# Eight of sixteen terms of a head-attention sum taken over by identity products; an exponent bias on another engine; re-ordered queues

## The reference, cut to what matters

```
x = x + attn(layernorm(x))         # head attention, below
x = x + xattn(layernorm(x), ctx)   # 16 heads, all 2048 keys, fake-quantised
x = x + ffn(layernorm(x))          # 8 experts, top 2, and a shared one
```

```
scores = einsum('bshd,bstd->bsht', q, k) / sqrt(16)   # h, t: heads; d: 16 features
probs  = softmax(scores, axis=-1)
attn   = einsum('bsht,bstd->bshd', probs, v) @ Wo.T
```

## Time and profile before

| | |
|---|---|
| median of 3 runs | 1065.17 us (1061.33 to 1065.57) |
| the profiled execution | 1068.14 us, span 1065.7 us |
| PE busy | 722.0 us (68%), 7072 products |
| DVE busy | 906.5 us (85%), 1841 instructions |
| ACT busy | 737.3 us (69%), 989 |
| POOL busy | 746.9 us (70%), 728 |
| mean granted TensorE clock | 0.838 |

### The profile page before, as it was taken

The page is one execution under the profiler, slowest core; times in us unless marked ns, Lnnn a source line. Parts: engine busy times, 40 slices in busy tenths (PEclk is TensorE's granted clock), DMA queues, the critical chain, the costliest instruction groups (busy, mean ns, idle before and its releaser), DMA issues. The chain is left out here.

```text
span 1065.7 us, 21210 instructions
## 1 busy us (share of the span) xinstructions
PE 722.0 (68%) x7072; PEld 388.6 (36%) x7072; DVE 906.5 (85%) x1841; ACT 737.3 (69%) x989; POOL 746.9 (70%) x728
## 2 busy tenths in 40 slices
PE   6966647666675867675776758576667767675674
PEld 4543323333342524343332425243333324242333
DVE  3887769989888899989898989899888989999851
ACT  2644656868677776868686877778686868878742
POOL 6688987787786778787886868787878868730000
PEclk9975777888896978889897989888878979798965
DMA  6012767979698896979797999979697979999981
GB/s 225 1 40 70 133 119 140 186 115 192 128 176 147 150 173 127 187 114 198 120 194 144 160 168 146 190 121 188 129 179 115 192 150 169 172 167 182 162 161 25
DMA packets 574019, 156.01 MB, mean 146 GB/s; under 512 B 567252, under 2 KB 571863, under 8 KB 573527
## 3 DMA queue, kind: packets, MB, share of 16 engines
q1 hardware_dynamic: 573910, 154.67, 81.5%
HBM read 9.93 MB, written 2.10 MB: 11 GB/s over the span
## 5 line engine op out<-in xcount | busy, mean ns | idle before, releaser
L1135 DVE TENSOR_SCALAR_CACHE_REDUCE score<-ps_score,q_neg 128x1024 f32<-128x1024 f32 x512 | 636.2, 1277 | 17.2 <-PE ps_score L1459 15.9
L824 ACT ACTIVATE prob<-score,exp_bias 128x2048 uint16<-128x2048 f32 x256 | 512.1, 2001 | 61.4 <-DVE exp_bias L1145 58.5
L1459 PE MATMUL ps_score<-keys,queries 128*128 128x512 bf16 x1024 | 368.1, 450 | 255.4 <-DVE score L1135 248.7
L1459 PEld LDWEIGHTS ps_score<-keys,queries 128*128 128x128 bf16 x1024 | 72.2, 103 | 445.7 <-DVE score L1135 415.9
L527 POOL TENSOR_TENSOR product<-hs_exp,v_tok 128x1024 f32<-128x1024 f32 x64 | 149.4, 2347 | 31.0 <-ACT hs_exp L789 30.8
L534 POOL TENSOR_TENSOR product<-product 128x512 f32<-128x512 f32 x128 | 159.5, 1262 | 0.0
L527 POOL TENSOR_TENSOR product<-qk_rot 128x1024 f32<-128x1024 f32 x64 | 150.2, 2349 | 0.3 <-POOL qk_rot L520 0.2
L1489 PE MATMUL ps_pv<-prob_t,values 128*32 128x128 f16 x4096 | 74.2, 229 | 25.1 <-DMA prob_t<-prob 24.8
L545 POOL TENSOR_TENSOR product<-product 128x512 f32<-128x512 f32 x64 | 80.8, 1271 | 5.9 <-POOL product L534 5.9
L1489 PEld LDWEIGHTS ps_pv<-prob_t,values 128*32 128x32 f16 x4096 | 63.2, 101 | 55.2 <-issue 55.2
L466 POOL TENSOR_SCALAR var_eps<-mean_var 128x1 f32<-128x1 f32 x48 | 12.6, 262 | 90.2 <-DVE mean_var L1080 89.2
(11 more groups left out here) (124 smaller groups left out, 1112.2 us busy)
## 6 DMA issues: line engine op xcount, KB each, us to landing
prob_t<-prob SPq DMA_TRANSPOSE x256, 4.5
prob_t<-in_w SPq DMA_DIRECT2D x3, 1024.0 KB, 4.8
x_in<-in_x SPq DMA_DIRECT2D x16, 128.0 KB, 3.0
score<-in_cond_t SPq DMA_DIRECT2D x4, 512.0 KB, 6.3
out<-x_out SPq DMA_DIRECT2D x16, 128.0 KB, 2.7
w_qkv<-in_w_qkv SPq DMA_DIRECT2D x1, 768.0 KB, 4.4
early<-in_w_kv SPq DMA_DIRECT2D x1, 512.0 KB
w_s<-in_w_s SPq DMA_DIRECT2D x3, 128.0 KB
```

The costliest lines, as they stand in the source:

```text
L824: act.activation(prob[:, s, :].bitcast(U16), score[:, s, :], ACT.Exp, bias=exp_bias[:, s:s + 1], scale=-1.0, accum_out=prob_sum[:, t.par, ...
L1135: dve.tensor_scalar(score[:, s, HALF * i:HALF * i + HALF], ps_score[:, score_slot(t.count(H, h), i)].rearrange("p b k -> p (b k)"), q_neg[ ...
L1459: mm = pe.matmul(ps_score[:, score_slot(n, i), b, :], queries[:, t.par, h // 2, h % 2, :], keys[:, h // 2, k0:k0 + KEYS], start=True, stop ...
```

## The change

It has three parts.

1. The sums. GpSimd still multiplies, and folds each group of 16 terms to 8 (`fold`, eight times). `fold_8`, `fold_4` and `fold_2` are gone. TensorE adds the eight terms left: `sum_terms(i, t)` multiplies the identity with the eight slices `product[:, two slots, :, d]` (128 columns each, fp32, 16 elements or 64 bytes apart) and accumulates them in PSUM, four calls of eight products a tile. The sums lie in the second half of `ps_pv` (of bank 7 for the first two tiles). `sum_terms(0)` and `(1)` are at h = 14, `(2)` at h = 5, `(3)` at h = 7. GpSimd does not read PSUM in this kernel, so `shift_scores` and `norm_ho` go to VectorE, at h = 14 and h = 7.
2. The bias. `bias(h, t)` (256 in all) moves from VectorE to GpSimd, with the same operation on 128 x 1 and the waits for both halves' minima and for the buffer. Its places among GpSimd's products and folds are written out.
3. The order. Steps of all five queues are moved by one or a few heads: `load_x` from h = 15 to 10, the gather of `x_in` from 0 to 1, `ln_gather(1)` from 8 to 9, TensorE's `xq` and VectorE's `largest_query` and `quantise_queries` from 12, 12 and 13 to 14, `choose` from 10 to 11, `cross_sum` from 0 to 4, all four value products of tile n to the start of body t, and so on. The head scores of the second tile are finished ahead of the loop, as are its maximum and exponential.

```diff
-            def bias(h, t):
-
-                dve.wait_ge(score_kept, t.count(2 * H, 2 * h + 2))
...
+            def bias(h, t):
+                pool.wait_ge(score_kept, t.count(2 * H, 2 * h + 2))
+                pool.sem_inc(settled, 1)
+                if (due := t.due(H, h - RING + 1)) is not None:
+                    pool.wait_ge(prob_ready, due)
+                    pool.sem_inc(settled, 1)
+                s = h % RING
+                pool.tensor_scalar(exp_bias[:, s:s + 1], low[:, s, 0:1], low[:, s, 1:2], LN255, ALU.min, ALU.add
+                    ).then_inc(bias_ready, 1)
...
+            def fold(i, t):
+
+                terms = product[:, i % 4]
+                pool.wait_ge(multiplied, t.count(8, i + 1))
+                pool.sem_inc(settled, 1)
+                pool.tensor_tensor(terms[:, :, 0:HD // 2], terms[:, :, 0:HD // 2], terms[:, :, HD // 2:HD],
+                                   ALU.add
+                    ).then_inc(folded, 1)
...
+            def shift_scores(t):
+                dve.wait_ge(hs_shift, t.count(2, 1))
+                if (due := t.due(1)) is not None:
+                    dve.wait_ge(hs_exped, due)
+                dve.tensor_tensor(hs[:], heads(sums_of(t)), over(hs_max[:], H), ALU.subtract).then_inc(hs_shift, 1)
+
+            def norm_ho(t):
+                dve.wait_ge(summed, t.count(4, 4))
...
+                dve.tensor_tensor(ho_n[:], heads(sums_of(t)), over(hs_inv[:], HD), ALU.mult).then_inc(ho_done, 1)
...
+            def wait_pv():
+
+                if read["shift"] > 0:
+                    pe.wait_ge(hs_shift, 2 * read["shift"])
+                if read["ho"] > 0:
+                    pe.wait_ge(ho_done, read["ho"])
+                if read["xo"] > 0:
+                    pe.wait_ge(xo_kept, read["xo"])
+
+            def sum_terms(i, t):
+
+                pe.wait_ge(folded, t.count(8, 2 * i + 2))
...
+                    wait_pv()
+                out = sums_of(t)[:, P * (i % 2):P * (i % 2) + P]
+                for d in range(HD // 2):
+                    mm = pe.matmul(out, ident[:], product[:, 2 * (i % 2):2 * (i % 2) + 2, :, d], start=d == 0,
+                                   stop=d == HD // 2 - 1)
+                mm.then_inc(summed, 1)
...
-                    if (t + 3).exists() and h == 15:
+                    if (t + 3).exists() and h == 10:
                         load_x(t + 3)
```

More of the change, by code:

```diff
@@ new lines, in body @@
+                if t.exists():
+                    bias(11, t)
+                    bias(12, t)
+                if a.exists():
+                    score_products(3, a)
+                    fold(3, a)
+                if t.exists():
+                    bias(13, t)
+                    bias(14, t)
+                    bias(15, t)
+            def all_scores(t):
+                for j in range(0, G, 2):
+                    score_products(j, t)
+                    score_products(j + 1, t)
+                    fold(j, t)
+                    fold(j + 1, t)
@@ L976, in _ @@
             keep_values(3)
+            head_exp(second)
             over_tiles(body)
@@ new lines, in body @@
+                    if a.exists() and h == 1:
+                        loaded(a)
+                        ln_gather(0, x_in[:, a.par, :], a)
+                    if m.exists() and h == 11:
+                        choose(m)
+                    if o.exists() and h == 3:
+                        expert_hidden(1, o)
+                    if n.exists() and not t.starts() and h == 1:
+                        sum_scores(n)
+                    if t.starts() and h == 5:
+                        sum_scores(n)
@@ L1289, in _ @@
                     ln_combine(0, second)
-                if u == 4:
                     largest_score(first)
+                    shift_scores(first)
                 if u == 5:
@@ L1308, in _ @@
             keep_first_values(1)
+            largest_score(second)
+            shift_scores(second)
             over_tiles(body)
@@ L1585, in body @@
                     if t.exists():
-                        scores(h, 0, t)
-                    if n.exists() and h == 11 + late:
-                        ln_turn(1, n)
-                    if m.exists() and h == 5:
-                        times_values(3 * G, m)
+                        scores(h, 1, t)
+                    if a.exists() and h == 14:
+                        sum_terms(1, a)
+                    if m.exists() and h == 11:
+                        gate_and_shared(1, m)
+                    if a.exists() and h == 5 + behind:
+                        queries_or_keys(1, a)
@@ new lines, in body @@
+                    if o.exists() and h == 2:
+                        experts(1, 0, o)
+                    if n.exists() and h == 12 + late:
+                        ln_turn(1, n)
+                    if m.exists() and h == 6:
+                        xo_project(m)
+                    if o.exists() and h == 1:
+                        experts(0, 0, o)
+                    if o.exists() and h == 3:
+                        experts_out(o)
+                    if o.exists() and h == 2:
+                        experts(1, 1, o)
```

482 lines of the change are left out of this document (207 added, 275 removed).

## The result

The changed kernel takes 1089.68 us in the median of 4 runs (1088.64 to 1091.67), the kernel before 1064.5 beside it (1061.33 to 1065.57). The ratio is 1.0244, 95% interval 1.0216 to 1.0272: 2.4% slower, where 1029 us was forecast. The profiled execution has a span of 1089.9 us.

What follows compares the result with a forecast made beforehand. VectorE was taken to set the pace: a floor of 51.6 us plus added terms made 57.1 a tile, 1.8 less. 23 us over 13 tiles, 8 at the start and 5 at the end gave 1032, median 1029; range 980 to 1086.

Steps and rivals of the forecast that it cites:

- (e): TensorE's four sum calls a tile, at 0.13 us a record, make VectorE wait 3.3 us a tile.
- Rival C: TensorE's reads 64 bytes apart are slow, 1.57 times: 61.9 us a tile, median 1091 us; chance 0.18.
- The ends: Outside the full tiles: 8 us gained at the start from GpSimd's shorter queue, 5 us in tiles 14 and 15.
- (g): After `choose` the clock falls to half and slows `xq` right before the quantisation: 2.3 us a tile added.
- (c): Sixteen biases a tile leave VectorE, one per head: 3.1 us a tile saved.
- (a): `x_in` loaded at h = 10 and read one head later: VectorE's wait of 2.9 us a tile ends.
- (b): VectorE's wait for the head attention's projection, 2.0 us a tile, goes as GpSimd's folds go.
- (f): The projection's new chain, `keep_ho` on ScalarE behind head 6's exponential, gives 0.6 us a tile of wait back.
- (d): `shift_scores` and `norm_ho` come to VectorE: 0.7 us a tile added, no block by GpSimd assumed.
- (h): `choose` on VectorE, blocked by GpSimd in nearly every tile, meets shorter instructions: 0.7 us a tile saved.
- D: Rival: biases come late behind GpSimd's instructions, two a tile costing 1 us each; median 1052 us; chance 0.15.

Runs made afterwards that it cites:

- e11: Changed kernel, full result, product tile laid out so TensorE reads neighbouring columns and GpSimd writes 256 bytes apart: 1010.77 us, ratio 0.9489 to the kernel before.
- e2: Changed kernel with identity products reading 128 neighbouring columns, so other terms are added: 1008.91 us, ratio 0.9464 to the kernel before.
- e8: The same kernel as e11 (changed kernel, neighbouring columns for TensorE, GpSimd writing 256 bytes apart), in one execution: 1012.91 us.
- e12: The kernel of e11 with the choice of experts one head later, h = 12 in place of 11: 1013.04 us, ratio 0.9496 to the kernel before.
- e3: The kernel before with one edit, `x_in` loaded at h = 10 in place of 15: 1031.75 us, ratio 0.9676.
- e4: The changed kernel with all biases back on VectorE, none on GpSimd: 1095.03 us, ratio 1.0269 to the kernel before.
- e9: The kernel of e11 with all biases back on VectorE: 997.23 us, ratio 0.9354 to the kernel before.
- e5: As e2, but with the columns 8 bytes apart, one timed execution: 1010.88 us.
- e6: As e2, but with the columns 16 bytes apart, one timed execution: 1101.74 us.
- e7: Changed kernel, full result, neighbouring columns for TensorE, GpSimd's loops turned to read score keys 64 bytes apart: 1017.53 us, ratio 0.9538 to the kernel before.

## Why the prediction was wrong, step by step

**The step that failed is (e), TensorE's sums.** It took 0.13 us a record from a product with neighbouring columns, said that no row showed one with columns 64 bytes apart, and chose the near row all the same. Measured: 0.217. Four calls hold TensorE for 13.9 us a tile, not 8.5. The exposed part was forecast at 3.3 us; it is 7.6. The waits stand where the step put them, larger: 2.2 us before the maximum (forecast 1.2, with the queries' turn), 1.6 before `norm_ho` (0.7), 3.7 before scores (1.4). With neighbouring columns a record takes 0.111 and VectorE's waits for scores are 1.9 us a tile (23.6 us in 700 of e11): the mechanism was right, its price was not.

**Rival C named the cause, with 0.18.** Its factor, 1.57, was drawn from ScalarE's strided copy; measured against neighbouring columns (e2) it is 0.217 / 0.111 = 1.95. Its 1091 us, beyond the end of the prediction's own range of 980 to 1086, lies 1 us from the result, but by luck, by two errors against each other: it had 61.9 us a tile (59.9 measured) and 13 us gained at the ends, where 11.7 were lost. The argument set against it, that an fp32 product takes its columns at half a bf16 one's rate, fails: the penalty came in full. Together with the Trainium skill's rule of the 16-byte line (Advanced Engine Details and Errata, SBUF Cachelines), which spoke for C, it should have had the larger chance.

**The ends.** 8 us were to be gained at the start; 17.4 were lost. The step saw GpSimd relieved and forgot that the key products of the start leave TensorE no room: its six calls hold it for some 21 us there. With neighbouring columns the first full tile is still at 151.5 to 154.0 (e8, e11, e12), 2.4 to 4.9 later than before, so this step was wrong in itself and not only by (e). How much of that is the sums and how much the new order, which puts the second tile's head scores ahead of the loop, no run separates. The last tiles gave 5.7 us, forecast 5.

**(g), the clock,** was wrong in its place and its length. The kernel after, behind one choice (448.66 us), PE, PEld, DVE, ACT, POOL busy, clock, DMA share, GB/s:

```profile
451.00:452.00 1.00, 0.00 (x0) 0.00 (x0) 0.96 (x3) 0.69 (x2) 0.78 (x2) 1.00 1.12 206
454.00:455.00 1.00, 1.00 (x12) 0.51 (x14) 1.00 (x3) 1.00 (x3) 0.29 (x1) 0.56 0.89 198
455.00:456.00 1.00, 1.00 (x44) 1.00 (x40) 1.00 (x1) 1.00 (x4) 0.00 (x0) 0.50 0.90 281
458.00:459.00 1.00, 1.00 (x6) 0.62 (x4) 1.00 (x3) 1.00 (x4) 1.00 (x1) 1.00 1.15 142
```

There is still a quiet stretch, and the clock still falls, but for some 3.5 us where it fell for some 10 before, and it is back when `xq` starts (457.95): its four records of 256 columns last 1.03 us, the price at full clock. Behind the next choice (508.95) it doesn't fall at all. Over 155 to 960 us it is 0.97 against 0.85 before. So `xq` costs nothing extra in these two tiles, and the 2.3 us a tile go from the sum, which then gives 54.8 for a kernel with cheap sums; e11 shows 55.1, though (c) below says that not every term was right for itself.

**(a)** was right: 2.9 us a tile forecast, 2.6 by e3 (34 / 13). **(b), (f)** were right: 2.0 goes and 0.6 comes back; measured 5.3 / 13.4 = 0.4 us. **(d), (h)** were about right: the two instructions take 0.42 us each, without a block; the second instruction of the choice fell from 2.26 to 1.19 us in the median, the first rose from 0.38 to 0.59, so -0.9 (forecast -0.7). Without biases on GpSimd they take 0.16 and 0.17 (e4): the biases' places in GpSimd's queue put part of the collision there.

**(c), the biases,** was right as work and wrong as time. 3.1 us of VectorE go, but a part comes back in the collision (1.4 us a tile between e4 and the kernel after, 2.3 between e9 and e11), and e9 against e11 says that the whole move costs 1.3 us a tile. D's mechanism, late biases and a bound that passes to other engines, was there with less weight than its 1052 us; in the kernel after it is hidden behind TensorE (e4).

Taken as a chain of measured kernels: before 1064.5; the early load, 1032; the sums on TensorE with neighbouring columns and the rest of the re-ordering, 997; the biases to GpSimd, 1011; the columns 64 bytes apart, 1090. No run separates the sums from the re-ordering.

## What to carry to other kernels

Before an operation moves to TensorE, look at the distance of the moving operand's columns: at 16 and at 64 bytes each record took twice as long as at 4 and 8, and the layout is to be turned on the side that does not mind (here GpSimd's writes). A cost that no row shows is to be priced by the row that shares its access pattern, not by the one that shares its engine and shape. And a step taken off a busy engine need not be a gain: it can come late from the engine that it goes to, and move that engine's other work into the way. Measure each part of a compound change alone, since here two of the four steps of the chain above were losses and one small part, a load issued five heads earlier, gave as much (34 us) as the sums with the better layout and all other re-ordering together.

## What the runs showed of the hardware

- TensorE, fp32, 128 columns from SBUF, full clock, per record: columns 4 bytes apart 0.111 us (e2), 8 bytes 0.113 (e5), 16 bytes 0.226 (e6), 64 bytes 0.217 (kernel after).
- GpSimd multiplying 128 x 1024 fp32: writes 256 bytes apart 2.36 to 2.38 us, neighbouring writes 2.35 to 2.36; with one operand, the keys, read 64 bytes apart 2.55 (e7).
- ScalarE's copy of 128 x 256 fp32 to `v_tok`: 0.60 us with writes 64 bytes apart (e11), 0.37 with neighbouring writes (e7).
- A VectorE instruction of 8 columns with one SBUF input is held by GpSimd too, 1.84 us in e11 in place of 0.16 (e4). The Trainium skill (GPSIMD Engine Reference, Specifications) names, beside instructions with two SBUF inputs, those in a two-port mode; the trace agrees with a block of this kind. The rule on two inputs does not fit this instruction; whether it ran in a two-port mode no run shows. The earlier trace rows had shown the one with two inputs only.
